# A kernel of four graph networks: degree rows of six chunks loaded at once in the last network's first pass, and the stores of matrix tiles moved out of a layer's last chunk

## The reference

```python
x = x + L0_gnn(h)   # sum over edges, two products, log_softmax
x = x + L1_gnn(h)   # two GCN convolutions
x = x + L2_gnn(h)   # four layers: z = A h + h; relu(z W1 + b1) W2 + b2; batch norm over nodes; relu
x = x + L3_gnn(h)   # MixHop: for j = 0, 1, 2: (A^j)(h W_j + b_j), joined; batch norm; relu; MixHop again; product
```

## Time and profile before

| | us |
|---|---|
| median of 3 runs | 1291.31 (1289.57 to 1295.53) |
| the profiled execution | 1287.21 |
| its span | 1285.7 |
| TensorE busy | 1142.8 (89%) |
| VectorE busy | 686.6 (53%) |
| ScalarE busy | 455.5 (35%) |
| mean granted TensorE clock | 0.964 of full |

### The profile page before, as it was taken

One profiled execution on the slowest core, in us unless ns is written; L12 is line 12 of the kernel. 1 busy time (PEld: TensorE's weight loads), 2 busy tenths in 40 slices (PEclk: granted clock), 3 DMA queues, 4 the chain that ended last, 5 costly groups with the idle time before them and its releaser, 6 DMA issues.

```text
span 1285.7 us, 19418 instructions
## 1 busy us (share of the span) xinstructions
PE 1142.8 (89%) x6308; PEld 661.6 (51%) x6308; DVE 686.6 (53%) x2175; ACT 455.5 (35%) x1348; POOL 8.5 (1%) x31
## 2 busy tenths in 40 slices
PE   1677899999989999997997997994689998999997
PEld 1556677665645645544445454453435554444644
DVE  8999999994552235453454362546234324532211
ACT  1558988885661122102113113017111113631100
POOL 1000000000000000000000000000000000000000
PEclk9998899999999999998998998995899998999999
DMA  3000000001001000134233232329992313410001
GB/s 70 24 2 2 2 2 10 2 2 46 6 11 24 23 1 1 39 74 93 50 72 68 64 72 56 84 26 237 241 237 91 91 33 84 111 47 23 15 24 29
DMA packets 208801, 70.31 MB, mean 55 GB/s; under 512 B 180999, under 2 KB 208074, under 8 KB 208699
## 3 DMA queue, kind: packets, MB, share of 16 engines
q1 hardware_dynamic: 120267, 42.03, 14.6%
q10 hardware_dynamic: 88432, 27.02, 9.8%
HBM read 20.71 MB, written 28.26 MB: 38 GB/s over the span
## 4 chain that ended last, share of the span: by engine, by line
PE 75%; DVE 12%; ACT 5%; DMA 3%; issue 3%; ACTq 1%; DVEq 1%; POOL 0%; POOLq 0%; SPq 0%
PE PS L1156 49%; PE PS L886 7%; DVE HPb L750 4%; PE PS L1453 3%; PE PS L2408 3%; PE PS L875 2%; DMA HPb<-s_d 2%; PE PS L851 2%; PE PS L1907 2%; DVE HPb L701 2%; PE PS L1913 2%; ACT HPb L2385 1%; PE PS L1390 1%; ACTq L1795 1%; PE PS L1943 1%
## 5 line engine op out<-in xcount | busy, mean ns | idle before, releaser
L1156 PE MATMUL PS<-ADJ,HPb 125*128 125x500 bf16 (+2 forms) x2450 | 488.6, 355 | 7.5 <-DVE HPb L1964 3.0
L1156 PEld LDWEIGHTS PS<-ADJ,HPb 125*128 125x128 f16 x2450 | 240.0, 98 | 251.6 <-issue 38.1
L922 ACT CAST ADJ<-PS 126x72 f32 (+7 forms) x784 | 193.1, 315 | 51.6 <-PE PS L886 18.4
L1156 PE MATMUL PS<-ADJ,Zf 125*128 125x500 bf16 (+2 forms) x1050 | 202.1, 352 | 0.0
L886 PE MATMUL PS<-HPb 128*128 128x150 bf16 (+3 forms) x784 | 192.4, 347 | 3.1 <-ACT ADJ L922 2.3
L1156 PEld LDWEIGHTS PS<-ADJ,Zf 125*128 125x128 f16 x1050 | 102.3, 97 | 93.8 <-issue 1.3
L750 DVE TENSOR_SCALAR HPb<-XRf,Zf 128x176 bf16<-128x176 f16 (+2 forms) x588 | 134.4, 288 | 1.2 <-PE PS L886 0.7
L875 PEld LDWEIGHTS PS<-HPb 128*128 128x128 bf16 x642 | 86.3, 141 | 60.1 <-issue 34.4
L1700 DVE CUSTOM_DVE_ANT_0 HPb<-ADJ,HPb 125x625 bf16<-125x625 bf16 x125 | 101.2, 810 | 3.7
L875 PE MATMUL PS<-HPb 128*128 128x25 bf16 x642 | 90.8, 214 | 12.7 <-DVE HPb L750 12.0
L1808 DVE TENSOR_SCALAR Zf<-PS,B_L 128x500 f32<-128x500 f32 (+2 forms) x28 | 19.1, 682 | 141.8 <-PE PS L1913 141.8
(11 more groups left out here) (322 smaller groups left out, 1017.8 us busy)
## 6 DMA issues: line engine op xcount, KB each, us to landing
adj_d<-ADJ ACTq DMA_DIRECT2D x25, 700.0 KB
HPb<-y_d SPq DMA_DIRECT2D x19, 187.5 KB, 2.5
HPb<-di_d SPq DMA_DIRECT2D x10, 250.0 KB, 3.4
adj_d<-ADJ ACTq DMA_DIRECT2D x25, 81.2 KB
ADJ<-in_x SPq DMA_DIRECT2D x1, 1562.5 KB
q_d<-HPb SPq DMA_DIRECT2D x25, 62.5 KB
HPb<-di_d SPq DMA_DIRECT2D x5, 305.2 KB
HPb<-di_d ACTq DMA_DIRECT2D x5, 250.0 KB, 5.7
```

Source lines behind the costliest of these rows:

```text
L922: e.copy(to, WPS[group % BANKS][0:PD, t0 * RESTS[q]:t1 * RESTS[q]] .rearrange("p (t d) -> p t d", t=t1 - t0)).then_inc(s_mv, 1)
L1156: mm = e.matmul(accs[q], H[0:PN, t, q, 0:P], cols, start=(t == 0 and (two or q == 0)), stop=(t == NT - 1 and (two or q == 1)), skip_group_ ...
```

## The change

Two parts. First, `keep` now stores tile l * 6 + c in chunk c of layer l for the first six chunks, and tile 24 in addition in layer 0's chunk 2, so that no tile is stored in a layer's last chunk. Second, in L3's first pass the degree rows of chunks 0 to 5 are all loaded by SyncE before the third transposed load. They lie in the part of Zf that the next chunk's HB will fill (`beside(c)`), so SyncE waits first until TensorE has turned all blocks out of Zf. `red` reads the row from there and writes GAT. y1 of chunk k goes to the same place (`y1_of`) and not into LOS, so the next s1 can be loaded as soon as y1 is formed. The ReLU tiles go to GAT and not to HID. Only chunk 6 still gets its degree row in GAT, from ScalarE's queue. The rows of s1 have a semaphore of their own, `s_row`.

```diff
             def layer2(l, last):
...
-                        if base + c < NT:
-                            keep(base + c)
+                        if c < NC - 1:
+                            keep(l * (NC - 1) + c)
+                        if (l, c) == (0, 2):
+                            keep(NT - 1)
...
+            def beside(c):
+                return Zf[:, SPANS3[c + 1][0] * P:] if c + 1 < NC else GAT
+            def y1_of(c):
+                return beside(c) if c + 1 < NC else LOS
...
             if sp:
+                e.wait_ge(s_bn["tr"], LAYERS * NB)
+                for c in range(NC - 1):
+                    row_in(beside(c), di_d, c, SPANS3)
                 for c in range(2, NC):
                     turned(c)
...
             if dve:
-                    e.wait_ge(s_dib, dib0 + 32 * n)
-                    e.scalar_tensor_tensor(out=w(GAT), in0=sums3(k), scalar=1 / LOW, in1=w(GAT),
+                    if k == 0:
+                        e.wait_ge(s_dib, dib0 + 16 * (NC - 1))
+                    if n == NC:
+                        e.wait_ge(s_row, 16 * (NC + 1))
+                    done(E3["tt"], k)
+                    e.scalar_tensor_tensor(out=w(GAT), in0=sums3(k), scalar=1 / LOW, in1=w(beside(k)),
                                            op0=ALU.mult, op1=ALU.mult).then_inc(E3["red"], 1)
                     done(E3["d1"], n)
-                    e.scalar_tensor_tensor(out=w(LOS), in0=w(LOS), scalar=B_L3[:, R_B1, 1:2], in1=w(PS[:, 1, :]),
+                    if n < NC:
+                        e.wait_ge(s_row, 16 * n)
+                    e.scalar_tensor_tensor(out=w(y1_of(k)), in0=w(LOS), scalar=B_L3[:, R_B1, 1:2], in1=w(PS[:, 1, :]),
...
             if act:
                 done(E3["hp"], NB)
-                row_in(GAT, di_d, 0, SPANS3)
                 e.wait_ge(s_dout, 118)
-                row_in(LOS, s1_d, 0, SPANS3)
+                row_in(LOS, s1_d, 0, SPANS3, s_row)
                 for k in range(NC):
-                    done(s_y0, 16 * k)
-                    if k:
-                        done(E3["red"], n)
+                    done(E3["y"], n)
+                    store(1, k, y1_of(k), SPANS3, s_y)
+                    if n < NC:
+                        row_in(LOS, s1_d, n, SPANS3, s_row)
+                    done(E3["tr"], n)
                     for m, j in enumerate(tiles_of(k, SPANS3)):
-                        e.activation(HID[0:PN, m * P:(m + 1) * P], tile_of(XR, j), ACT.Relu, bias=NBU[0:PN, j:j + 1],
+                        e.activation(GAT[0:PN, m * P:(m + 1) * P], tile_of(XR, j), ACT.Relu, bias=NBU[0:PN, j:j + 1],
...
-                    done(E3["y"], n)
-                    store(1, k, LOS, SPANS3, s_y)
-                    if n < NC:
-                        done(E3["tr"], n)
-                        done(E3["d1"], n)
-                        row_in(GAT, di_d, n, SPANS3)
                     done(E3["z"], n)
+                    done(s_y, 16 * k)
...
                     done(E3["tt"], n)
+                    done(s_y0, 16 * k)
                     e.copy(first_of(HID, k, SPANS3), first_of(PS[:, 3, :], k, SPANS3)).then_inc(E3["he"], 1)
-                    if n < NC:
-                        done(s_y, 16 * n)
-                        row_in(LOS, s1_d, n, SPANS3)
+                    if n == NC - 1:
+                        row_in(GAT, di_d, n, SPANS3, s_row)
```

More of the change, by code:

```diff
@@ L120, in build @@
     KEPT = PN // 16 * 16
-    assert NT * NP <= NT * AW and KEPT < PN
+    assert NT * NP <= NT * AW and KEPT < PN and LAYERS * (NC - 1) + 1 == NT
     TURNED, s0 = [], 0
@@ L329, in build @@
         s_dout, s_dib, s_inv = sem("s_dout"), sem("s_dib"), sem("s_inv")
-        s_dt, s_home = sem("s_dt"), sem("s_home")
+        s_dt, s_home, s_row = sem("s_dt"), sem("s_home"), sem("s_row")
         s_first = sem("s_first")
@@ L2057, in store, with row_in @@
                 e.dma_start(y_d[q][:, j0 * PN:(j0 + nt) * PN], first_of(tile, c, spans)).then_inc(sem, 16)
-            def row_in(tile, v, c, spans):
+            def row_in(tile, v, c, spans, to=s_dib):
                 j0, nt = spans[c]
-                e.dma_start(first_of(tile, c, spans), bcast(v[j0 * PN:(j0 + nt) * PN])).then_inc(s_dib, 16)
+                e.dma_start(first_of(tile, c, spans), bcast(v[j0 * PN:(j0 + nt) * PN])).then_inc(to, 16)
+            def beside(c):
+                return Zf[:, SPANS3[c + 1][0] * P:] if c + 1 < NC else GAT
+            def y1_of(c):
+                return beside(c) if c + 1 < NC else LOS
             if sp:
@@ L2112, in layers @@
                     done(E3["agg"], n)
-                    e.wait_ge(s_dib, dib0 + 32 * n)
-                    e.scalar_tensor_tensor(out=w(GAT), in0=sums3(k), scalar=1 / LOW, in1=w(GAT),
+                    if k == 0:
[4 more added lines that the diff above has]
+                    e.scalar_tensor_tensor(out=w(GAT), in0=sums3(k), scalar=1 / LOW, in1=w(beside(k)),
                                            op0=ALU.mult, op1=ALU.mult).then_inc(E3["red"], 1)
                     done(E3["d1"], n)
-                    e.scalar_tensor_tensor(out=w(LOS), in0=w(LOS), scalar=B_L3[:, R_B1, 1:2], in1=w(PS[:, 1, :]),
+                    if n < NC:
+                        e.wait_ge(s_row, 16 * n)
+                    e.scalar_tensor_tensor(out=w(y1_of(k)), in0=w(LOS), scalar=B_L3[:, R_B1, 1:2], in1=w(PS[:, 1, :]),
                                            op0=ALU.mult, op1=ALU.add).then_inc(E3["y"], 1)
                     done(E3["y"], n)
-                    y_stats(1, k, LOS, SPANS3)
+                    y_stats(1, k, y1_of(k), SPANS3)
                     done(E3["tr"], n)
@@ L2186, in turned_h @@
                     for m in range(nt):
-                        mm = e.transpose(PS[:, 3, m * PN:(m + 1) * PN], HID[0:PN, m * P:(m + 1) * P], IDF[0:PN, 0:PN])
+                        mm = e.transpose(PS[:, 3, m * PN:(m + 1) * PN], GAT[0:PN, m * P:(m + 1) * P], IDF[0:PN, 0:PN])
                     mm.then_inc(E3["tt"], 1)
@@ L2285, in joined @@
                     e.tensor_tensor(first_of(GAT, c), sums(c, c, 4)[0], first_of(GAT, c), ALU.add).then_inc(E3b["red"], 1)
-                    e.wait_ge(s_dib, dib0 + 32 * NC + 16 * n)
+                    e.wait_ge(s_dib, dib0 + 16 * (NC - 1) + 16 * n)
                     done(E3b["red"], n)
```

## The result

| | before | after |
|---|---|---|
| median, us | 1290.44 (4 runs, 1286.18 to 1295.53) | 1274.50 (4 runs, 1271.57 to 1276.86) |
| profiled execution, us | 1287.21 | 1276.86 |
| span, us | 1285.70 | 1275.3 |

The ratio is 0.9874 with a 95% interval of 0.9832 to 0.9916: 16.3 us faster, between 10.8 and 21.7. The forecast was 14.0 us and 1277.3. Four runs on each side are few. All 53 runs of before on record, those made beside the experiments included, have a median of 1287.9 us, and all six of after 1276.0: 11.9 us less.

What follows compares the result with a forecast made beforehand. TensorE (89% busy) was taken to bound the kernel, so only its waits pay: 4.4 us at layer ends plus 9.6 in L3's first pass, 14.0 together, from the 1291.31 median to 1277.3; range 1271 to 1285.

Steps and rivals of the forecast that it cites:

- Layer ends: Last chunk of layers 0 to 2: without the store, the square root starts 0.44 us after the aggregate; 4.4 us gained.
- Stores moved: Layer 0's two-tile chunk 2 and layer 3's later stores are hidden by gaps and slack; cost 0, at most 1 us.
- Third load: L3's first pass: third transposed load issued 9.7 us later behind the six degree rows, whose bytes add 1.5 us.
- Landings of chunks 5 and 6: L3's first pass: the last two transposed loads land at 958.5 and 975.1, and TensorE waits for both.
- The rule of 16.6 us between landings: L3's first pass: sign of a right forecast, TensorE's waits before chunks 5 and 6 ended by loads landing 16.6 us apart.
- Row of s1: Chunk 1 of L3's first pass: TensorE waits 3.2 us for VectorE's z, behind the first s1 row landing in 7.6 us.
- Granted clock: TensorE's clock, if it falls in the new waits, would add up to 1.7 us each.
- The pass: L3's first pass: ends at 988.7 where it was near 998.3, so 9.6 us gained.
- A: Rival: transposed loads keep TensorE's pace, L3's first pass is bound by TensorE alone; 19.7 us gained, time 1271.6; 14%.
- B: Rival: rows drain in turn at 3.0 us, big loads start 25.5 us later; 1291.6, or 1284 with half that delay; 13%.
- C: Rival: slower; each row takes 5.7 us in turn, big loads start 41.6 us later, time 1307.6; 4%.
- D: Rival: only the layer part works, a store or row being late somewhere held to be hidden; 1287 to 1283; 9%.

Runs made afterwards that it cites:

- e1: The kernel before with only the stores of matrix tiles moved, L3's first pass unchanged: 1282.92 us, ratio 0.9953.
- e2: The changed kernel with the stores as before, so only the rows' part of the change: 1281.52 us, ratio 0.9944.
- e4: The changed kernel with the six early degree rows written to 8 of 128 partitions, scaling left out for the others: 1271.76 us, ratio 0.9859.
- e6: The changed kernel with the first row of s1 loaded by SyncE ahead of the first transposed load: 1273.23 us, ratio 0.9893.
- e3: The kernel before with SyncE waiting for all turned blocks ahead of the third transposed load, no row moved: 1284.95 us, ratio 0.9965.
- e5: The changed kernel with degree rows issued as their blocks are turned, the third transposed load behind four rows, two rows after it: 1275.27 us, ratio 0.9907.
- e7: The changed kernel with degree rows issued block by block and the first s1 row loaded ahead of the first transposed load: 1276.39 us, ratio 0.9908.

## Why the prediction was right, and where it was off

The mechanism held: both parts pay, and behind the wait for rows stands one for transposed loads. That the time came so near is in part luck. The stretches gave 11.1 us of the 14.0, the four timed runs of each 16.3, and all runs on record 11.9. By its steps:

- **Layer ends, 4.4 us.** The square root follows by 0.43 us as in layer 3 of before. The layers gave 4.3 us in the first pair, 4.9 in the means. e1 alone shows 2.8 in its trace and 6.1 by its ratio, on either side of it; over all 14 traces it is 4.7.
- **Stores moved, 0.** The first transposed load starts 4.2 us behind layer 3's aggregate (866.06, 870.26), where it was 1.1. e1 and e2 separate the parts: 4.2 us in e1, where the stores alone moved, 1.3 in e2, where they didn't. So the moved stores delay it. It is hidden by the slack to the third load, as said.
- **Third load 9.7 us later, 1.5 for the rows.** It was 7.5 us behind the point where the queue had issued all that stands ahead of the rows (886.64). The six issues took 3.72 us where I counted 2.2, at 0.36 each, so the load came 3.8 us behind the last turned block and not 2.2; its landing at 912.3 is 3.1 later than forecast. (Forecast times are moved by 1.8 us here, because the last ReLU ahead of the pass started 1.8 us earlier than in before.) The rows weigh more than 1.5 us: e4.
- **Landings of chunks 5 and 6, 956.7 and 973.3.** They were 959.2 and 970.7: the first 2.5 us late, the second 2.6 early. So one wait of 4.04 us in place of two of 2.8 and 3.0. The rule of 16.6 us between landings was too even; they were 15.5, 13.4, 18.0 and 11.5 us apart.
- **Row of s1, 3.2 us.** 2.32 us, since the row landed in 5.75 and not 7.6. The culprit was the wrong one: ScalarE's ReLU tiles behind a store, not VectorE's z. e6 took the wait away and moved the pass by less than its spread: the waits for loads grew by 1.9 us.
- **Granted clock.** The prediction named up to 1.7 us more behind each new wait, and put nothing of it into the sum. Behind the 4.04 us wait it was 1.7 us, the full bound. Behind the one in chunk 1 it was as much: ten matmuls, the pair of L2207 and 24 more took 8.10 us from 908.14, where the same took 6.42 in before. The 3.63 us wait that the prediction cites had cost a little less, 1.6 us.
- **The pass, 9.6 us.** This term was mis-sized. It measured 8.2 us in the same pair of traces, 1.4 less: chunk 5's load landed 2.5 late and the clock took 1.7 behind it, against the 3.0 of a wait before chunk 6 that did not come; 0.2 is left over. It measured 6.2 in the means, because the first trace of before had row waits of 15.0 us where the other two had 9.8 and 10.8. That a single execution sizes the term was the weakest point of the sum.

The forecast for the profiled execution was 1273.2 us, and it took 1276.86: 1.4 us from the pass, 0.1 from the layers and 2.5 from the stretch ahead, less 0.4 in the rest. The medians moved by more (16.3) than the stretches in the traces (11.1). The gap lies inside the interval, and against the 11.9 us of all runs on record it nearly goes: the first four runs of before have a median 2.6 us above that of all, and the first four of after one 1.5 below.

Of the rivals: A, a pass bound by TensorE alone, is out by the load waits in all three traces of after; e4, where most of the rows' bytes are gone and no load is waited for, shows what it would give: 83.6 us. B and C, rows that drain one after the other and a late start that cancels or turns the gain, are out by the trace of after: the six rows landed 3.3 to 6.0 us behind their issues, side by side, the last 9.3 us behind the first issue, and the first wait for a load was 0.49 us, before chunk 3. e3 adds that a later start costs nothing where rows are waited for, but it had no rows on that queue and a smaller delay, so it does not test them alone. D is out by e2.

## What to carry to other kernels

When a wait for a transfer goes, ask which transfer is next and count the bytes in front of it: here an earlier issue gave nothing that can be told from the spread (e5, e7), and fewer bytes brought the pass to 83.6 us (e4). A DMA of many small pieces (256 bytes each in the stores of matrix tiles) should not be issued ahead of a lone step on the path: its issue alone holds the queue, here two of them for 4.1 us. Size a wait for DMA from several traces of the same kernel; one trace may be at the edge of a spread (4.6 us here) that is over a quarter of the whole gain.

## What the hardware showed that I had not expected

- The same code's pass took 93.8, 95.8 and 98.4 us in three executions. Rows of one kind land in 7.57 and 9.43 us, in 5.0 to 5.8 in e3, and in 3.0 on a quiet queue. Where big loads are waited for instead, four passes of the same code lie within 2.5 us (87.7 to 90.2).
- A big transposed load holds the issuing queue for 11.4 to 20.8 us. What is issued behind it on that queue, however small, is late by that: in e5 the third load holds it from 888.89 to 904.67, and the next row is issued at 904.71.
- With a DMA share over 1, the rate was 210 GB/s in the window of e5 above (share 1.15), 262 and 267 in those of after (1.08, 1.23), and 290 while the loads had the engines to themselves (1.27). The share alone doesn't say what is moved.
- TensorE's clock fell to 1.2 GHz for a stretch behind waits of 2.32 and 4.04 us in after, but not behind those of 2.55 and 2.78 us in before. It cost 1.7 us in both.
- Starting the big loads later, with nothing else changed, made the kernel 4.5 us faster, 2.4 to 6.6 (e3); the cause is not shown.
